# Last layer of a spectral CNN: the third and fourth image pair go through the Fourier stages together, and the output is stored image by image

## The reference

```python
for j in range(4):
    z = conv3x3(x, Kj); z = batchnorm(z, gamma, beta); z = relu(z)
    z = conv3x3T(z, Kj)
    x = x + 0.1 * z
    x = batchnorm(x, gamma, beta)                     # moments over batch and image
    x = real(ifft2(fft2(x) * t[None]))                # t: a real table, 32 x 64 x 64
return x
```

## Time and profile before

| what | value |
|---|---|
| median of 3 runs | 667.3 us (663.94 to 668.04) |
| profiled execution, its own time | 662.35 us |
| its span, first to last instruction | 660.5 us |
| mean granted TensorE clock | 0.977 |
| PE busy | 616.0 us, 93% of the span |
| DVE busy | 499.6 us, 76% |
| ACT busy | 300.8 us, 46% |
| POOL busy | 236.7 us, 36% |
| written to HBM | 4.19 MB |

### The profile page before, as it was taken

How to read it: one execution, slowest core, us unless ns; L and a number is a source line. 1 busy time by engine, 2 the same in 40 slices (tenths; PEclk the granted TensorE clock), 3 DMA queues, 4 the chain that set the end, 5 groups by cost and what they waited for, 6 DMA issues and landing times.

```text
span 660.5 us, 14557 instructions
## 1 busy us (share of the span) xinstructions
PE 616.0 (93%) x5848; PEld 196.2 (30%) x5848; DVE 499.6 (76%) x946; ACT 300.8 (46%) x518; POOL 236.7 (36%) x183
## 2 busy tenths in 40 slices
PE   6598999989999999999999999999999999999883
PEld 4122333322323232223232222333322223333331
DVE  3679888876588877668887967689879676887674
ACT  1456666664494132237822433297214234941123
POOL 0367766674032443310525522033345220323300
PEclk9798999999999999999999999999999999999986
DMA  9997111122910022287002023940022249000026
GB/s 188 192 167 123 34 34 25 24 53 66 218 52 2 1 66 66 66 193 174 2 1 63 5 73 87 229 110 1 1 66 66 66 108 216 2 1 2 0 66 191
DMA packets 44466, 51.21 MB, mean 78 GB/s; under 512 B 36208, under 2 KB 36336, under 8 KB 42352
## 3 DMA queue, kind: packets, MB, share of 16 engines
q1 hardware_dynamic: 39792, 48.72, 34.0%
q10 hardware_dynamic: 4608, 1.56, 1.3%
HBM read 11.99 MB, written 4.19 MB: 25 GB/s over the span
## 4 chain that ended last, share of the span: by engine, by line
PE 82%; DVE 10%; issue 3%; ACT 1%; DMA 1%; SPq 1%; POOL 0%; DVEq 0%; ACTq 0%; POOLq 0%
PE psum L1124 47%; PE psum L1201 7%; PE psum L1274 5%; PE psum L1348 5%; PE psum L1305 4%; PE psum L1333 3%; DVE work L1025 3%; PE psum L1152 2%; PE psum L1330 2%; PE psum L1189 2%; PE psum L1232 1%; PE psum L1234 1%; DVE work L852 1%; DVE work L1060 1%; DVE spare L852 1%
## 5 line engine op out<-in xcount | busy, mean ns | idle before, releaser
L1124 PE MATMUL psum<-Z,wts 128*32 128x512 f32 x1536 | 173.2, 595 | 0.0
L1124 PE MATMUL psum<-X,wts 128*32 128x512 f32 x1536 | 171.9, 594 | 0.1
L493 POOL TENSOR_TENSOR Z<-X 128x512 f32<-128x512 f32 x64 | 81.9, 1303 | 219.2 <-DVE X L1001 218.1
L584 ACT ACTIVATE Z<-psum 128x512 f32<-128x512 f32 x64 | 38.1, 595 | 114.9 <-PE psum L1124 103.8
L512 POOL TENSOR_TENSOR X<-Z 128x1024 f32<-128x1024 f32 x24 | 57.0, 2398 | 88.2 <-DVE Z L1042 88.2
L648 ACT ACTIVATE Z<-Z,small 128x512 f32<-128x512 f32 (+4 forms) x92 | 80.3, 922 | 4.5 <-DVE small L964 4.0
L1124 PEld LDWEIGHTS psum<-X,wts 128*32 128x32 f32 x1536 | 46.5, 109 | 113.7 <-issue 110.2
L1124 PEld LDWEIGHTS psum<-Z,wts 128*32 128x32 f32 x1536 | 45.7, 109 | 112.6 <-issue 111.0
L870 DVE BATCH_NORM_STATS2 stats<-Z 128x6 f32<-128x512 f32 x60 | 41.1, 689 | 43.6 <-ACT Z L584 43.2
L669 ACT ACTIVATE work<-X,small 128x512 bf16<-128x512 f32 x64 | 45.5, 713 | 59.1 <-DVE X L1001 59.1
L1001 DVE SCALAR_TENSOR_TENSOR X<-psum,X 128x512 f32<-128x512 f32 x64 | 43.6, 682 | 24.1 <-PE psum L1124 22.7
(11 more groups left out here) (139 smaller groups left out, 849.3 us busy)
## 6 DMA issues: line engine op xcount, KB each, us to landing
X<-X SPq DMA_DIRECT2D x64, 260.0 KB, 3.8
Z<-Z SPq DMA_DIRECT2D x32, 520.0 KB, 9.0
Z<-x SPq DMA_DIRECT2D x36, 128.0 KB, 4.2
out<-Z SPq DMA_DIRECT2D x12, 256.0 KB, 4.0
parS<-par SPq DMA_DIRECT2D x4, 673.0 KB, 9.7
Z<-x SPq DMA_DIRECT2D x12, 120.0 KB, 5.3
Z<-x ACTq DMA_DIRECT2D x14, 64.0 KB, 4.2
Z<-x SPq DMA_DIRECT2D x14, 64.0 KB, 4.6
```

The costliest lines, as they stand in the source:

```text
L493: nc.gpsimd.tensor_tensor(rows(Z0, REG, bp, CH * (2 * half + i), CH), low, high, op=op)\
L1124: last = nc.tensor.matmul(out_b[C * r:C * r + C, :], weights[:, o:o + C], rows(src, reg, bp, g, CH, dj - 1), start=(dj == 0), stop=(dj == ...
```

## The change

In the last layer, pair 2's forward transform along W no longer stands between the last two chunks of the second convolution. Behind that convolution the list is new: pair 1's last stage first, then the two pairs 2 and 3 in each stage one right behind the other. So that they can be, pair 3 of the last layer gets buffers of its own, all in X2: the first 2048 columns for `freqw`, the next 2048 for `spec`, the next 2048 for its two turned halves. The four `affine` steps move too: those of pairs 0 and 1 stand behind the scaling of both pairs' spectra.

The store takes one image in an issue in place of one residue: all 128 partitions of Z2 on one side, and on the side of `out` an access pattern of 4 residues by 32 channels by the row lines. The last wait of SP counts accordingly.

```diff
@@ layer_steps
-        14: fourier(j, 2, "fwdW"),
+        14: fourier(j, 2, "fwdW") if j + 1 < DEPTH else [],
@@ last_steps
-    steps = [("slot0", j, 2)] + fourier(j, 2, "fwdH") + [("slot0c", j, 2), ("moments", j)]
-    steps += [("turn", j, BP - 1, 0), ("turn", j, BP - 1, 1), ("norm", j, 2), ("affine", j, 0)] + fourier(j, 3, "fwdW")
-    steps += fourier(j, 2, "invH") + [("slot0", j, 3)] + fourier(j, 3, "fwdH") + [("slot0c", j, 3)]
-    steps += fourier(j, 1, "invW") + [("back", j, 1, 0), ("back", j, 1, 1), ("affine", j, 1)]
-    steps += fourier(j, 2, "invW") + [("back", j, 2, 0), ("back", j, 2, 1)] + fourier(j, 3, "invH") + fourier(j, 3, "invW")
-    return steps + [("affine", j, 2), ("back", j, 3, 0), ("back", j, 3, 1), ("affine", j, 3)]
+    steps = fourier(j, 1, "invW") + [("back", j, 1, 0), ("back", j, 1, 1), ("moments", j)]
+    steps += [("turn", j, BP - 1, 0), ("turn", j, BP - 1, 1)] + fourier(j, 2, "fwdW") + fourier(j, 3, "fwdW") + [("norm", j, 2)]
+    for bp in (2, 3):
+        steps += [("slot0", j, bp)] + fourier(j, bp, "fwdH") + [("slot0c", j, bp)]
+    steps += [("affine", j, 0), ("affine", j, 1)] + fourier(j, 2, "invH") + fourier(j, 3, "invH")
+    for bp in (2, 3):
+        steps += fourier(j, bp, "invW") + [("back", j, bp, 0), ("back", j, bp, 1), ("affine", j, bp)]
+    return steps
@@ buffers
+        def beside(j, bp, t, i):
+            return X2[:, WORK * i:WORK * (i + 1)] if (j, bp) == (DEPTH - 1, BP - 1) else t[:, :]
+        def rows_of(j, bp):
+            return beside(j, bp, freqw, 0)
+        def spectrum(j, bp):
+            return beside(j, bp, spec, 1)
+        def turned_half(j, bp, half):
+            if (j, bp) == (DEPTH - 1, BP - 1):
+                return X2[:, 2 * WORK + 2 * N * half:2 * WORK + 2 * N * (half + 1)]
+            return turned[(2 * bp + half) % 3]
@@ store
-        def store(eng, bp, l, n):
-            for q in range(R):
-                to = out[2 * bp:2 * bp + 2].rearrange("i c (q l) w -> q c i (l w)", q=R)[q]
-                both = Z2[C * q:C * q + C, bp * REG2:bp * REG2 + 2 * G * W].rearrange("p (i x) -> p i x", i=2)
-                eng.dma_start(to[:, :, W * l:W * l + W * n], both[:, :, W * l:W * l + W * n]).then_inc(out_done, 16)
+        def store(eng, bp, first=0, n=G):
+            for b2 in range(2):
+                to = out[2 * bp + b2].rearrange("c (q l) w -> q c (l w)", q=R)[:, :, W * first:W * (first + n)]
+                o = bp * REG2 + b2 * G * W + W * first
+                eng.dma_start(to, Z2[:, o:o + W * n]).then_inc(out_done, 16)
```

More of the change, by code:

```diff
@@ L455, in _ @@
                 sp.wait_ge(x_back, NCH * (DEPTH - 1) + Q * bp + Q)
-                store(sp, bp, 0, G)
+                store(sp, bp)
             sp.wait_ge(x_back, NCH * DEPTH - Q + 2)
             store(sp, BP - 1, 0, G // 2)
-            sp.wait_ge(out_done, 16 * R * (BP + 1))
+            sp.wait_ge(out_done, 16 * 2 * (BP + 1))
         @block.gpsimd
@@ L674, in keep_slot0 @@
                 bk.full(n)
-                nc.scalar.activation(spec[:, :].rearrange("p (a s) -> p a s", s=SL)[:, :, 0], bank(n)[:, 0:2 * C],
+                nc.scalar.activation(spectrum(j, bp).rearrange("p (a s) -> p a s", s=SL)[:, :, 0], bank(n)[:, 0:2 * C],
                                      ACT.Identity).then_inc(drained[n % BANKS], 1)
@@ L1009, in turn @@
                 dve.wait_ge(halves_mixed, Q * (BP * j + bp) + 3 + half)
-                k, g = 2 * bp + half, 2 * CH
+                g = 2 * CH
                 o = bp * REG + g * GROUP * half
@@ L1013, in turn @@
                 for b in range(2):
-                    dst = turned[k % 3].rearrange("p (m b c) -> p b m c", b=2, c=C)
+                    dst = turned_half(j, bp, half).rearrange("p (m b c) -> p b m c", b=2, c=C)
                     last = nc.vector.transpose(dst[:, b], src.rearrange("p g (e l b) -> p b g e l", e=2, b=2)[:, b])
@@ L1024, in move_rows @@
                 src = psum[:, b0:b0 + R, :].rearrange("p r (g b c) -> p c b r g", b=2, c=C)[:, 8 * q:8 * q + 8]
-                nc.vector.transpose(freqw[:, N * q:N * q + N], src).then_inc(rows_moved, 1)
+                nc.vector.transpose(rows_of(j, bp)[:, N * q:N * q + N], src).then_inc(rows_moved, 1)
             def move_slots(j, c):
@@ L1053, in scale_fwdH @@
             def scale_fwdH(j, c):
-                n, q = NUMBER["fwdH", j, c], c % Q
+                n, (bp, q) = NUMBER["fwdH", j, c], divmod(c, Q)
                 bk.full(n)
@@ L1058, in scale_fwdH @@
                     .unsqueeze(2).broadcast_to([128, 8, 2, SL - 1])
-                to = spec[:, N * q:N * q + N].rearrange("p (c b s) -> p c b s", c=8, b=2)[:, :, :, 1:SL]
+                to = spectrum(j, bp)[:, N * q:N * q + N].rearrange("p (c b s) -> p c b s", c=8, b=2)[:, :, :, 1:SL]
                 nc.vector.tensor_tensor(to, src, tt, op=ALU.mult).then_inc(drained[n % BANKS], 1)
@@ L1272, in forward_w @@
                             k = slice(32 * r, 32 * r + 32)
-                            src = turned[(2 * bp + half) % 3][k].rearrange("p (g e m) -> p e g m", e=2, m=64)
+                            src = turned_half(j, bp, half)[k].rearrange("p (g e m) -> p e g m", e=2, m=64)
                             last = nc.tensor.matmul(bank(first + r)[64 * half:64 * half + 64, :],
@@ L1286, in slot_0 @@
                 pe.wait_ge(rows_moved, Q * (BP * j + bp + 1))
-                straight, crossed = (by_chunk(freqw[:, :].rearrange("p (a s) -> p a s", s=SL)[:, :, 0], x) for x in range(2))
+                straight, crossed = (by_chunk(rows_of(j, bp).rearrange("p (a s) -> p a s", s=SL)[:, :, 0], x) for x in range(2))
                 to = bank(n)[:, 0:2 * C]
@@ L1295, in forward_h @@
             def forward_h(j, c):
-                first, q = NUMBER["fwdH", j, c], c % Q
+                first, (bp, q) = NUMBER["fwdH", j, c], divmod(c, Q)
                 if q == 0:
-                    pe.wait_ge(rows_moved, Q * (BP * j + c // Q + 1))
+                    pe.wait_ge(rows_moved, Q * (BP * j + bp + 1))
                 for x in range(2):
@@ L1303, in forward_h @@
                         k, half = slice(64 * p, 64 * p + 64), 64 * (p ^ x)
-                        src = freqw[k, N * (q + x):N * (q + x) + N].rearrange("p (a s) -> p a s", s=SL)[:, :, 1:SL]
+                        src = rows_of(j, bp)[k, N * (q + x):N * (q + x) + N].rearrange("p (a s) -> p a s", s=SL)[:, :, 1:SL]
                         last = nc.tensor.matmul(bank(first + x)[half:half + 64, 0:16 * (SL - 1)], cstS[k, C_FH:C_FH + 64], src,
@@ L1327, in inverse_h @@
                 for x in range(2):
-                    src = spec[:, N * (q + x):N * (q + x) + N]
+                    src = spectrum(j, bp)[:, N * (q + x):N * (q + x) + N]
                     if j == DEPTH - 1:
```

## The result

The changed kernel takes 691.98 us (median of 4 runs, 690.3 to 692.21), the kernel before 665.65 in the same comparison: a ratio of 1.0387, 95% interval 1.0343 to 1.0432. It is 26 us slower. The profiled execution took 691.93 us, span 690.1.

The account below looks back on a forecast made before the run. PE, then PE and DVE waiting for each other, bound the kernel; stores were hidden but for 4 us. First store 640.8 + 0.9 + 44.6 + 1.1 = 687.4, 26.9 over 660.5; 667.3 + 26.9 = 694.2 us, range 687 to 710.

Parts of the forecast that it names:

- Four engines: New store: outermost count 4 in `out` lets only 4 of 16 DMA engines carry it; chance 0.79 within 687 to 710.
- The transfer's time: Stores: 4.19 MB on four engines at 23.5 GB/s each, 94 GB/s together, need 44.6 us.
- The first store: Tail: SP issues its first store at 640.8 and not at 633.4, 7.4 us later.
- The late normalisation chain: Tail: 2.1 us of small operations stand behind both row moves and end at 634.8, where before they ended at 630.9.
- The end of the computation: Tail: ACT ends the last `affine` at 653.8 against 656.1, 2.3 us earlier, with 1.5 us of uncertainty either way.
- The total: Whole kernel: median of before 667.3 plus 26.9 makes 694.2 us.
- The rival with 16 engines: Stores: inner counts are cut as well, so all 16 engines work; 666 us, up to 670; chance 0.16.
- The rival with slower engines: Stores: four engines at 13.6 GB/s each move 54.5 and need 77.0 us; 727 us; chance 0.05.
- the 218 GB/s of pair 0's stores: Kernel before, pair 0's stores: the 32 partitions that 16 engines read limited the rate, not the engines.
- some 34 us of waiting for the DMA: Sign in the profile after: the chain of waits ends in this wait.
- A share of 0.25 for over 40 us: Sign in the last slices: a quarter of 16 engines at 85 to 102 GB/s while PE, DVE and ACT are idle.
- 12 us or so: Tail: time between the first store and the end of computation, against 44.6 us that the stores need.

Follow-up runs that it names:

- experiment 4: Changed kernel, but the 128 rows of an image in `out` named as one dimension, so rows land in another order: 663.92 us, ratio 0.9975.
- experiment 3: Changed kernel, but each issue takes one image and two residues, 64 partitions, in twice as many issues: 731.94 us, ratio 1.1017.
- experiment 2: Kernel before with the new store alone, in the old order of steps: 687.52 us, ratio 1.0368.
- experiment 8: Kernel of experiment 1 with the normalisation and the affine steps of pairs 0 and 1 moved ahead of both row moves: 667.29 us, ratio 1.0019.
- experiment 10: Kernel of experiment 8, but pair 2 goes through to its store before pair 3's inverse stages: 666.04 us, ratio 1.0013.
- experiment 7: Kernel before with a store's four issues alternating, residues 0, 2, 1, 3 (2, 0, 3, 1 in pair 3's second half): 664.44 us, ratio 0.9988.
- experiment 1: Changed kernel's new order of steps and buffers with the old store, one residue of 32 partitions and two images an issue: 665.84 us, ratio 1.0012.
- experiment 5: Changed kernel storing only residues 0 and 1 (partitions 0 to 63), half the bytes: 691.98 us, one execution.
- experiment 6: Changed kernel storing only residues 1 and 2 (partitions 32 to 95), half the bytes: 689.32 us, one execution.
- experiment 12: Kernel of experiment 2 with each residue's 32 rows following each other in `out`, so rows land in another order: 685.83 us, ratio 1.0334.

## Why the prediction was right

**Four engines.** This carried the forecast, and it held wherever it was tried: 132 packets an issue, a share of 0.25, and 385 to 390 GB/s as soon as the outermost count alone was changed (experiment 4), with two engines at a count of 2 (experiment 3). Engines followed the outermost count in `out`, up to 16, at 2, 4, 32 and 128. The Z2 side never had the smaller count, so that both sides count alike was argued and not run.

**The transfer's time.** 44.6 us were foretold and the packets moved for about 44.5 (from a us behind 643.49 to 689.0). That is luck in part: two errors cancel. The rate of an engine was put at 23.5 GB/s, between 21.5 and 25.5; it is 26 once steady, above my upper end. With that, 4.19 MB take 40.3 us. The other 4 us are the slow first stretch at 41 to 66 GB/s, the 94 GB/s from 680 to 688 us, and an end at which the share falls to 0.12 (45 GB/s at 688 us); I had none of them.

**The first store.** Foretold at 640.8, or 23.3 behind chunk 14's addition; measured 24.1. The late normalisation chain (its last operation begins at 637.29; it ends 18.2 behind the addition and was to end at 17.3), both spectra ahead of `affine`, both as worked out. The 0.8 us are PE's `fwdW` of pair 3, which took 3.72 us and not 2.83. It ran wholly at a granted clock of 0.50, behind 3.3 us of idleness, where before it ran at 0.85 in its first half and at 0.50 in its second, behind 2.0 us. The prediction let a stage of 2.0 grow to 2.8 at most; `fwdH` of pair 2 took 3.61 too, at 0.50. In the trace's own time the store came at 643.49, and 1.9 us of the lateness lay ahead of the changed part.

**The end of the computation.** Foretold 36.3 behind the addition, measured 37.2; before 38.6. A gain of 1.4 us, not 2.3, for the same reason.

**The total.** 694.2 us were forecast and 691.98 measured. Of the 2.2 us, 1.65 are the median of before, 667.3 when I forecast and 665.65 in the comparison; the difference was put at 26.9 and is 26.3. By experiments: the store alone makes 22.2, the order alone 0.5 in the medians, and both together 26.3. The order costs more with the new store than without it, since it makes the first store 8.2 us later, and the stores never catch up. It got 3.6 of these us back, since its stores had one slow stretch and a dip where experiment 2's had three slow stretches (46.6 against 50.2 us from the first issue to the end); why, is open.

**The rival with 16 engines** was put at 666 us, up to 670, and at a span that ends 41.9 behind the addition at 344 GB/s. Experiment 4 is that kernel but for the places of the rows: 663.92 us and 42.2, with 385 to 390 GB/s. Its deciding point was named rightly, the last two pairs' stores in a bunch; experiments 8, 10 and 4 show it, with the bunch, without it, and with it at the higher rate. **The rival with slower engines** (13.6 GB/s each) fell: an engine moves 26 GB/s. The runs fit the prediction's reading that the 218 GB/s of pair 0's stores is set by the partitions that an issue reads: the same 16 engines pass 385 to 390 when it reads 128 (experiment 4), and the alternation leaves that rate sooner (experiment 7).

**What was wrong in the list of signs.** I expected some 34 us of waiting for the DMA at the end of the chain of waits. The chain ends on ACT's last operation, and SP's final wait is 14.3 us, since SP is held while it issues (below). Whoever looks for this stall in the chain alone will not find it. Two more signs were misjudged. A share of 0.25 for over 40 us while nothing computes contradicts the prediction's own sums, which end the computation at 653.8 and the packets at 686.3; the engines were idle for some 33 us. And the cover it put at "12 us or so" is 13.0 by its own times and 13.1 as measured.

## What to carry to other kernels

When a store or a load is rewritten so that one issue covers more, write down the outermost count of both access patterns. Here the smaller one, up to 16, was the number of engines; a count that does not divide 16, and a small count on the SBUF side, were not run. All 128 partitions on the SBUF side do not help against a leading 4 on the DRAM side. Compute against the whole volume: hidden transfers stay hidden only while their rate times the cover is enough, and here 13 us of cover at 104 GB/s hide 1.4 MB of 4.19. And before two units are made to finish together, see what they both need at the end.

## What the runs showed of the hardware

- **An issue is held when few engines carry it.** The line of the store in the changed kernel (durations min/median/max in ns):

```profile
L419 SPq DMA_DIRECT2D out<-Z x8: 562/2926/7256, 643.5 to 669.4; - x8
```

  In the kernel before it was

```profile
L402 SPq DMA_DIRECT2D out<-Z x16: 315/432/1272, 633.4 to 656.2; - x16
```

  With four engines an issue took up to 7.3 us of SP's time, with 16 up to 1.3. ACT's two issues took up to 1.1 us, no more than with 16 engines (1.3 in experiment 1), but in experiment 3, with two engines, one took 5.7 and SP's up to 12.1. On a queue that also computes, this could cost more than the transfer; no run here shows it.
- **Slow stretches of a stream on few engines.** For about 5 us behind the first issue, 2 or 4 engines move about half of what they move later (26 against 52 GB/s, 41 to 66 against 104), at nearly the same share. Neither the partitions read (experiments 5 and 6) nor the places written (experiment 12) explain it. Two more such stretches come in experiments 2 and 12, some 15 and 43 us behind the first issue in both, the second while nothing computes; the changed kernel has only the dip near 684. This stays open.
- **Stores to HBM at 385 to 390 GB/s** when an issue reads all 128 partitions with 16 engines (experiment 4), against 205 to 218 when it reads 32.
